# FFN weights split by ScalarE and GpSimd and turned by DMA during the attention; shared groups one unit per slot in steps 16 to 18

## The chip, the cores and the metric

The kernel runs on one core of one Trainium2 chip. The metric is the device time in microseconds of one execution. The core has TensorE (PE: matrix products, and transposes as products with an identity), VectorE (DVE), ScalarE (ACT), GpSimd (POOL) and SyncE (SP, which in this kernel issues nearly all DMAs). Each engine runs its own program in order. They wait for each other on semaphores alone, and every wait, buffer and address is written out by hand.

## The reference

64 sequences of 64 tokens of width 128 (4096 tokens), each with a context of 128 rows. All in float32:

```python
x = x + xattn(layernorm(x), ctx)      # 16 heads of 8, then Wo, layer norm with gamma and beta
x = x + attn(layernorm(x))            # one causal head of 128, then Wo
x2n = layernorm(x)
gates, idx = top_k(x2n @ gate_w.T, 2); gates = softmax(gates)       # 8 experts
shared   = silu(x2n @ shared_w1.T) @ shared_w2.T                    # hidden width 512
selected = sum over the two experts e of a token:
           gate * (silu(x2n @ experts_w1[e].T) @ experts_w2[e].T)   # hidden width 512
x = x + shared + selected
```

The 18 weight matrices of the last part (8 experts and the shared one, two each) have 128x512 elements. The products of the FFN need them with the other dimension on the partitions than they have in memory, so each must be transposed ("turned"), and each is kept as two float16 tiles, a high part W_hi and a rest W_lo, scaled by 256. A product of the FFN is three float16 products: W_hi by x_hi, W_hi by x_lo, W_lo by x_hi.

## The kernel before, in words

The tokens stand in 32 tiles of 128, two tiles to a **half** (four sequences), so there are 16 halves. **Step** h of the attention works on half h: `most_steps` calls `step` for h from -3 to 17, and step 18 is called by itself. A step has eight **slots** (`UNITS`), two heads in each: TensorE makes the scores twice (once for the row maximum, DVE's `m_bf` L902, and once transposed for the exponential), ScalarE makes the exponential `p` (L680) and its float16 part `p_hi` (L685), and the rest `p_lo` (L356) is made by POOL in slots 1, 4 and 6 (`ON_POOL`) and by DVE in the others. POOL takes up its part at the start of the slot after. Around this, the slots do smaller work for other halves, each piece at a fixed slot in the table `MISC`: the transposes and projections of halves h+1 and h+2, output and layer norm of half h-1 (`yn`, `x1n`, `x1T`), and the second attention of half h-2 (`qk`, `s`, `pT`, `z`). The layer norms' roots run on POOL (`root`, L524 and L526) and the normalised rows are made by DVE (L805). In steps 16, 17 and 18 there are no scores any more, and only this smaller work is left, a chain in which each engine hands on to the next. Its last result is `x2n` of half 15, which step 18 makes: a high and a low part, turned by two DMA transposes into `x2T`.

SP's queue, for half h (`turn`): x rows two halves ahead, the context one ahead, then `q_parts` to DRAM (L390), the two halves of `k_parts` to DRAM (L393), and 16 pairs of small loads that bring them back stacked by head (`Qs` L408, `Ks` L409); between these, `x2_rows` turns `x2n` of an older half (L424).

Routing is done in four parts of the tokens, after steps 11, 15 and 17 and, for the last four tiles (part `LAST`), after step 18: TensorE makes the logits (L1203) and counts ranks, DVE works out for each token the two rows `row_no` of a list in DRAM, and POOL sends the tokens' rows there, 64 indirect DMAs in all (L537), 56 of them in the slots of steps 11 to 18 (table `SENT`), eight at the end. SP writes padding rows behind each expert's list (L470), from places that DVE has worked out (`pad0`), and then fetches blocks of 256 rows, transposing them into `xT` (L481).

The FFN runs in **units** of 128 of the 512 hidden columns: "up" is 3 products of 512 columns on TensorE (L1311), silu (L742) and `h_hi` (L745) on ScalarE, `h_lo` (L991) on DVE, and "down" is 12 products of 128 columns on TensorE (L1324). A unit's up stands three units (`AHEAD`) before its down in TensorE's order. The shared expert has 8 groups of 512 tokens with 4 units each (32 units); the routed part has 40 blocks of 256 rows with 2 units each (each unit then takes 256 of the hidden columns). POOL scatters a block's result to DRAM (L617, the 80 indirect DMAs), and it is read back (`yt`) and added at the end.

The 18 weights are loaded by SP, turned by TensorE in steps 16 and 17, four products each (L1235), into four PSUM banks; ScalarE writes W_hi from there (L658) and DVE W_lo (L812). `weights_at` says which matrices belong to a slot: one a slot at first, then two. Then come the first two shared groups (8 units), step 18, the routing of the last part, 16 more shared units, the 80 routed units, and the last 8 shared units.

## Time and profile before

| | |
|---|---|
| median of 3 runs | 634.56 us (634.42 to 635.3) |
| the profiled execution | 632.83 us |
| its span (first to last instruction) | 631.1 us |
| busy: TensorE, VectorE, ScalarE, GpSimd | 481.8, 469.4, 399.6, 336.7 us |
| mean granted clock of TensorE | 0.917 of full speed |

The 1.7 us between the profiled execution and its span lie before the first and behind the last instruction. No engine is busy for the whole span: the busy shares are means over stages that have different limits, so the kernel must be read stage by stage. The attention steps 0 to 15 take from about 40 to 389 us, steps 16 to 18 with the routing behind them from there to about 456, and the routed part from about 480 to the end.

### The profile page before, as it was taken

The page shows a single profiled execution, that of the slowest core. Times are in us where ns is not written, and L with a number is a line of the kernel's source. Part 1 is how long each engine was busy: PE and PEld are TensorE (multiplying, and loading weights), DVE is VectorE, ACT ScalarE, POOL GpSimd, SP SyncE. Part 2 cuts the span into 40 slices and gives each one's busy share as a digit, 9 for nine tenths or more (in the row PEclk, how much of TensorE's full clock was granted, in tenths as well). Part 3 has the DMA queues.
Part 4 walks back from the last instruction along what each step waited for, and adds up shares of the span by engine and source line. Part 5 has one row for each costly group of instructions (what it writes and reads, how often), then busy time and mean ns, then how long its engine had stood idle before and what let it go on. Part 6 is the DMA issues. An engine that isn't in the chain of part 4 may idle for free.

```text
span 631.1 us, 18436 instructions
## 1 busy us (share of the span) xinstructions
PE 481.8 (76%) x5770; PEld 396.6 (63%) x5770; DVE 469.4 (74%) x1417; ACT 399.6 (63%) x767; POOL 336.7 (53%) x486
## 2 busy tenths in 40 slices
PE   4488888778877887858877776558579999999960
PEld 1277677666666666646665665455358888888840
DVE  4258999998899999977877878575566666666644
ACT  2257777766777677644666653346669888888840
POOL 2213554355346444525777775755041888878842
PEclk9998999998999999976889986777879999999985
DMA  3453433444354455322543500344132453534349
GB/s 100 109 126 80 115 103 98 96 99 109 96 100 97 98 103 102 95 72 60 109 101 94 130 31 22 116 132 122 27 103 48 93 95 82 96 72 91 45 128 273
DMA packets 166703, 61.09 MB, mean 97 GB/s; under 512 B 116547, under 2 KB 163415, under 8 KB 166628
## 3 DMA queue, kind: packets, MB, share of 16 engines
q1 hardware_dynamic: 161968, 51.65, 36.1%
q0 software_dynamic: 4640, 8.48, 4.9%
q8 instruction: 42, 0.69, 0.5%
q14 instruction: 33, 0.27, 0.2%
q10 hardware_dynamic: 20, 0.01, 0.0%
HBM read 28.40 MB, written 23.28 MB: 82 GB/s over the span
## 4 chain that ended last, share of the span: by engine, by line
PE 31%; DVE 23%; issue 19%; POOL 13%; SPq 4%; ACT 4%; DMA 3%; DVEq 1%; POOLq 0%; ACTq 0%
PE bank L1311 8%; PE bank L1324 7%; DVE p_lo L356 3%; POOL listed L537 3%; DVE O_tok L887 3%; DVE m_bf L902 2%; POOL results L617 2%; POOL rstd L526 2%; PE bank L1160 2%; DVE st L794 2%; POOL p_lo L356 2%; PE bank L1151 2%; PE bank L1288 1%; SPq L408 1%; PE bank L1269 1%
## 5 line engine op out<-in xcount | busy, mean ns | idle before, releaser
L680 ACT ACTIVATE p<-bank 128x512 f32<-128x512 f32 x128 | 76.2, 595 | 60.8 <-PE bank L1255 26.2
L991 DVE TENSOR_TENSOR h_lo<-h,h_hi 128x512 f16<-128x512 f32 x112 | 77.3, 692 | 42.7 <-ACT h_hi L745 41.7
L902 DVE TENSOR_REDUCE m_bf<-bank 128x4 bf16<-128x512 f32 x128 | 86.9, 679 | 22.4 <-PE bank L1269 21.3
L1324 PE MATMUL bank<-W_hi,h_hi 128*128 (+1 forms) x448 | 83.1, 222 | 13.7 <-DVE h_lo L991 13.7
L617 POOL DMA_INDIRECT results<-y_sb,row_info x80 | 79.3, 991 | 19.4 <-issue 17.6
L356 POOL TENSOR_TENSOR p_lo<-p,p_hi 128x512 f16<-128x512 f32 x48 | 56.7, 1181 | 56.2 <-ACT p_hi L685 55.9
L537 POOL DMA_INDIRECT listed<-rows_of,row_no x64 | 63.9, 998 | 38.9 <-DVE row_no L875 23.5
L685 ACT ACTIVATE p_hi<-p 128x512 f16<-128x512 f32 x128 | 80.6, 630 | 5.5
L1324 PE MATMUL bank<-W_lo,h_hi 128*128 (+1 forms) x448 | 82.7, 222 | 0.0
L1324 PE MATMUL bank<-W_hi,h_lo 128*128 (+1 forms) x448 | 82.7, 222 | 0.0
L742 ACT ACTIVATE h<-bank 128x512 f32<-128x512 f32 x112 | 66.7, 596 | 23.7 <-PE bank L1311 18.9
L524 POOL TENSOR_TENSOR vpe<-mv,eps 128x2 f32<-128x2 f32 x64 | 15.1, 236 | 112.3 <-DVE mv L798 112.1
L745 ACT ACTIVATE h_hi<-h 128x512 f16<-128x512 f32 x112 | 70.5, 630 | 3.5
L1288 PE MATMUL bank<-V_hi,p_hi 128*128 128x17 f16 x512 | 51.1, 174 | 19.2 <-POOL p_lo L356 12.5
L1311 PE MATMUL bank<-xT,W_hi 128*128 128x256 f16 x320 | 57.1, 274 | 3.8 <-ACT h L742 1.9
L1288 PEld LDWEIGHTS bank<-V_hi,p_hi 128*128 128x128 f16 x512 | 42.9, 98 | 26.4 <-POOL p_lo L356 15.5
L356 DVE TENSOR_TENSOR p_lo<-p,p_hi 128x512 f16<-128x512 f32 x80 | 57.6, 720 | 0.7 <-ACT p_hi L685 0.7
L1324 PEld LDWEIGHTS bank<-W_hi,h_hi 128*128 128x128 f16 x448 | 44.4, 99 | 20.1 <-issue 15.3
L1269 PE MATMUL bank<-Ks,Qs 128*128 128x128 f16 x512 | 52.8, 230 | 4.3 <-DMA Ks<-k_rows 4.3
L1250 PEld LDWEIGHTS bank<-neg_ident,m_bf 128*128 128x128 bf16 x512 | 42.4, 104 | 18.6 <-issue 5.2
L1250 PE MATMUL bank<-neg_ident,m_bf 128*128 128x128 bf16 x512 | 53.3, 231 | 0.6 <-DVE m_bf L902 0.6
L1255 PE MATMUL bank<-Qs,Ks 128*128 128x256 f16 x256 | 52.6, 290 | 0.0
(198 smaller groups left out, 1367.0 us busy)
## 6 DMA issues: line engine op xcount, KB each, us to landing
k_rows<-k_parts SPq DMA_DIRECT2D x32, 256.0 KB, 2.7
Ks<-k_rows SPq DMA_DIRECT2D x128, 64.0 KB
ctx_in<-in_ctx SPq DMA_DIRECT2D x16, 256.0 KB, 3.2
Qs<-q_rows SPq DMA_DIRECT2D x128, 32.0 KB
w_in<-in_L_ffn_experts_w SPq DMA_DIRECT2D x16, 256.0 KB, 4.3
yt<-results SPq DMA_DIRECT2D x16, 256.0 KB, 5.2
x_all<-in_x SPq DMA_DIRECT2D x16, 128.0 KB, 2.7
q_rows<-q_parts SPq DMA_DIRECT2D x16, 128.0 KB, 2.0
```

Of the source, the lines that this page charges most:

```text
L356: eng.tensor_tensor(p_lo[:, s % 4, :], p32[:, s % 2, :], p_hi[:, s % 4, :], ALU.subtract).then_inc(low_of(h, s)[0], 1)
L537: pool.indirect_dma_start(out=listed[:, :], out_offset=bass.IndirectOffsetOnAxis(ap=row_no[:, n, t:t + 1], axis=0), in_=rows_of[:, t, n, : ...
L617: pool.indirect_dma_start(out=results[:, :], out_offset=bass.IndirectOffsetOnAxis(ap=row_info[b][:, t, 0:1].bitcast(U32), axis=0), in_=y_s ...
L680: act.activation(p32[:, s % 2, :], T_ps[s % 2][:, :], ACT.Exp, scale=XSCALE).then_inc(exp_done, 1)
L685: act.activation(p_hi[:, s % 4, :], p32[:, s % 2, :], ACT.Copy).then_inc(p_hi_done, 1)
L745: act.activation(h_hi[k % RING][:, :], h32[k % RING][:, :], ACT.Copy).then_inc(hhi_done, 1)
L902: dve.tensor_reduce(m_bf[:, slot, :], M_ps[s % 2][:, :].rearrange("p (n k) -> p n k", k=SK), AX.X, ALU.max).then_inc(max_done, 1)
L991: dve.tensor_tensor(h_lo[k % RING][:, :], h32[k % RING][:, :], h_hi[k % RING][:, :], ALU.subtract).then_inc(hlo_done, 1)
L1250: pe.matmul(T_ps[s % 2][:, n * P:n * P + P], m_bf[:, r * UNITS + s, n:n + 1].broadcast_to([P, P]), neg_ident[:, :], start=(n == 0), stop=F ...
L1288: last = pe.matmul(PV_ps[p][:, hd * VW:hd * VW + VW], pp[:, sv % 4, w0:w0 + P], vv[rv][:, p, hd, :], start=(m == 0), stop=(m == 2))
L1311: last = pe.matmul(U_ps[k % RING][:, c * width:c * width + width], ww[:, w(c)], xx[part], start=(m == 0), stop=(m == 2))
L1324: last = pe.matmul(y[:, t * D:t * D + D], hh[k % RING][:, cols], ww[:, w(c)], start=(first and c == 0 and t == 0 and m == 0), stop=(end an ...
```

## The change

- **Loading and turning.** TensorE's transposes, their PSUM banks and the two evacuations are gone. From step -1 on, each step takes one matrix: SP loads it (`load_weight`, into one of two `w_in` buffers), ScalarE scales it in place at the end of slot 1 (`weights_scaled`) and makes the float16 part at the end of slot 6 (`weights_hi`), POOL makes the rest at slot 7, behind its `p_lo` of slot 6 and ahead of `xb`, and two steps later SP turns both by two DMA transposes of 128x512 float16 (`turn_weight`), between the context load and the writes of q and k. The 18 steps are -1 to 16. The shared expert's two matrices are first (`W_ORDER`).
- **Shared units.** From slot 3 of step 16 on, each slot ends with one shared unit on TensorE, ScalarE and DVE: units 0 to 4 in step 16, 5 to 12 in step 17, 13 to 20 in step 18 (`shared_at`, `FILL_FROM`, `FILLED` = 21). Units 21 to 31 follow; the logits of the last part stand behind unit 23, the ranks behind 25, DVE's stages of routing behind 23, 24, 25 and 26 (`ROUTE_AT`). All 32 come ahead of the routed blocks, and none is left behind them.
- **SP's tables.** Padding waits for `pad0` alone, which DVE now makes first, and SP loads eight registers with one instruction (`rows_at`) instead of one before each DMA.
- **End.** After the last block DVE goes straight to the sums of the read-back results.

```diff
-WEIGHTS_FROM = HALVES * 8 + 2
+WEIGHTS_AT = 1
+FILL_FROM = HALVES * UNITS + 3
+FILLED = (HALVES + 3) * UNITS - FILL_FROM
+ROUTE_AT = (23, 24, 25, 26)
+W_ORDER = (2 * E, 2 * E + 1) + tuple(range(2 * E))
...
-        w_in = sb("w_in", [P, 4, CH, P])
+        w_in = sb("w_in", [P, 2, CH, P])
+        w_split = sb("w_split", [P, 2, 2, HID], F16)
...
+        def weight_step(h):
+
+            return not isinstance(h, int) or 0 <= h + WEIGHTS_AT < 2 * NE
+
+        def weight_ring(h, r):
+
+            return (1 - r, 8 * h + (8 * r + 16), 16 * h + 16 * r)
+
+        def shared_at(h, s):
+
+            n = h * UNITS + s - FILL_FROM if isinstance(h, int) else -1
+            return range(n, n + 1) if n >= 0 else range(0)
...
+            def load_weight(k):
+                e, second = weight_of(k)
+                w = ((ew1, ew2)[second][e] if e < E else (sw1, sw2)[second])
+                need(sp, wt_lo, k - 1)
+                sp.dma_start(w_in[:, k % 2, :, :],
+                             w.rearrange("d (c h) -> d c h", h=P) if second else w.rearrange("(c p) d -> p c d", p=P)
+                             ).then_inc(w_loaded[k % 2], 16)
+
+            def turn_weight(k):
+
+                e, second = weight_of(k)
+                sp.wait_ge(wt_lo, k + 1)
+                for part, dst in enumerate(((W2_hi, W2_lo) if second else (W1_hi, W1_lo))):
+                    sp.dma_start_transpose(dst[:, e * HID:e * HID + HID].rearrange("p (c n) -> p c n", c=CH),
+                                           w_split[:, k % 2, part, :]).then_inc(turned[k % 2], 16)
...
+                if h >= 2:
+                    turn_weight(h - 2)
+                load_weight(h)
...
+                    if s == 7 and weight_step(h):
+                        q = weight_ring(h, r)[0]
+                        pool.wait_ge(wt_hi, h + (WEIGHTS_AT + 1))
+                        pool.tensor_tensor(w_split[:, q, 1, :], w_in[:, q, :, :].rearrange("p c d -> p (c d)"),
+                                           w_split[:, q, 0, :], ALU.subtract).then_inc(wt_lo, 1)
...
+            def weights_scaled(h, r):
+
+                q, loads, turns = weight_ring(h, r)
+                act.wait_ge(w_loaded[q], loads)
+                act.activation(w_in[:, q, :, :], w_in[:, q, :, :], ACT.Copy, scale=WSCALE).then_inc(wt_scaled, 1)
+
+            def weights_hi(h, r):
+
+                q, loads, turns = weight_ring(h, r)
+                act.wait_ge(wt_scaled, h + (WEIGHTS_AT + 1))
+                need(act, turned[q], turns)
+                act.activation(w_split[:, q, 0, :], w_in[:, q, :, :].rearrange("p c d -> p (c d)"),
+                               ACT.Copy).then_inc(wt_hi, 1)
...
-                    for n in weights_at(h, s):
-                        weights_hi(n)
+                    if s == 1 and weight_step(h):
+                        weights_scaled(h, r)
+                    if s == 6 and weight_step(h):
+                        weights_hi(h, r)
+                    for n in shared_at(h, s):
+                        unit(n, n)
...
+            def rows_at(table_, last):
+
+                return nc.values_load_multi_w_load_instructions(table_, engines=[mybir.EngineType.SP], min_val=0, max_val=last)[1]
...
-            sp.wait_ge(tables_ready, 3)
-            for e in range(E):
-                first = sp.value_load(pad0[0:1, e:e + 1], min_val=0, max_val=E * REGION - BR)
+            sp.wait_ge(tables_ready, 1)
+            for first in rows_at(pad0[0:1, 0:E], E * REGION - BR):
...
+                firsts = rows_at(row0[0:1, i * LB:i * LB + LB], E * REGION)
+                for b, first in enumerate(firsts):
...
+            for n in range(FILLED, ROUTE_AT[3] + 1):
+                shared_unit(n)
+                for stage in {ROUTE_AT[0]: (0,), ROUTE_AT[1]: (1,), ROUTE_AT[2]: (2, 3), ROUTE_AT[3]: (5,)}.get(n, ()):
+                    route(LAST, stage)
...
+            block_out(BLOCKS // LB - 1, LB - 1)
+            for g in range(FG):
+                routed_in(g)
...
-            def weights(n):
-
-                pe.wait_ge(w_loaded[n % 4], 16 * (n // 4 + 1))
-                need(pe, wt_lo, n - 3)
-                if n < 4:
-                    pe.wait_ge(max_done, UNITS * HALVES)
-                    pe.wait_ge(norm_done, PAIRS * HALVES)
-                for c in range(CH):
-                    last = pe.transpose(W_ps[n % 4][:, c * P:c * P + P], w_in[:, n % 4, c, :], ident[:, :])
-                last.then_inc(wt_pe, 1)
...
+                if n == 0:
+                    pe.wait_ge(exp_done, UNITS * HALVES)
+                    pe.wait_ge(max_done, UNITS * HALVES)
+                    pe.wait_ge(norm_done, PAIRS * HALVES)
+                    for r in range(2):
+                        pe.wait_ge(turned[r], 32)
+                    for ahead in range(AHEAD):
+                        shared_up(ahead)
...
-            pe.wait_ge(exp_done, UNITS * HALVES)
-            pe.wait_ge(wt_lo, 2 * NE)
-            for n in range(AHEAD):
-                shared_up(n)
-            shared_before(0, EARLY * CH)
             step(HALVES + 2, 0)
-
-            pe.wait_ge(x2T_in, 32 * HALVES)
-            for name in ("x1T", "z"):
-                pe.wait_ge(ev[name], HALVES)
-            logits(LAST)
-            ranks(LAST)
-            shared_before(EARLY * CH, N0)
+            for n in range(FILLED, N0):
+                shared_unit(n)
+                if n == ROUTE_AT[0]:
+                    pe.wait_ge(x2T_in, 32 * HALVES)
+                    for name in ("x1T", "z"):
+                        pe.wait_ge(ev[name], HALVES)
+                    logits(LAST)
+                if n == ROUTE_AT[2]:
+                    ranks(LAST)
```

The two loops `for n in shared_at(h, s)` stand at the same place, the end of a slot, in the programs of TensorE, ScalarE and DVE; on TensorE and DVE they call `shared_unit`.

How the order moves, at three places. **POOL, from slot 7 of step 15 to the root of the output norm in step 16**, before. `xb` is half 15's residual with a bias, the L537 rows are sends, `yg` and `x_1` belong to half 15:

```order
L356 TENSOR_TENSOR p_lo<-p,p_hi 128x512 [waits v_done,p_hi_done]
L574 TENSOR_TENSOR xb<-x_all,bcast 128x256 [waits x1_done,x_in]
L537 DMA listed<-rows_of,row_no 35072x130 [waits placed,rows_copied]
L537 DMA listed<-rows_of,row_no 35072x130
L524 TENSOR_TENSOR vpe<-mv,eps 128x2 [waits normed_x2,stat_x2]
L526 TENSOR_TENSOR rstd<-vpe,minus_half 128x2 [waits vpe_x2]
L537 DMA listed<-rows_of,row_no 35072x130 x6
L524 TENSOR_TENSOR vpe<-mv,eps 128x2 [waits normed_y,stat_y]
L526 TENSOR_TENSOR rstd<-vpe,minus_half 128x2 [waits vpe_y]
```

The same place after (L555 are the sends):

```order
L360 TENSOR_TENSOR p_lo<-p,p_hi 128x512 [waits v_done,p_hi_done]
L574 TENSOR_TENSOR w_split<-w_in,w_split 128x512 [waits wt_hi]
L597 TENSOR_TENSOR xb<-x_all,bcast 128x256 [waits x1_done,x_in]
L555 DMA listed<-rows_of,row_no 35072x130 [waits placed,rows_copied]
L555 DMA listed<-rows_of,row_no 35072x130
L542 TENSOR_TENSOR vpe<-mv,eps 128x2 [waits normed_x2,stat_x2]
L544 TENSOR_TENSOR rstd<-vpe,minus_half 128x2 [waits vpe_x2]
L555 DMA listed<-rows_of,row_no 35072x130 x6
L542 TENSOR_TENSOR vpe<-mv,eps 128x2 [waits normed_y,stat_y]
L544 TENSOR_TENSOR rstd<-vpe,minus_half 128x2 [waits vpe_y]
L580 TENSOR_TENSOR yg<-yn,bcast 128x256 [waits normed_y]
L586 TENSOR_TENSOR x_1<-yg,xb 128x256 [waits ev_z,normed_x1,xb_done,yg_done]
```

The subtraction of one weight now stands between `p_lo` and `xb`, ahead of all the sends; it waits for ScalarE (`wt_hi`). In steps 0 to 14 it stands at the same place, between `p_lo` and `xb`.

**ScalarE, second half of step 17**, before. `V`, `P`, `rows_of` and `P2T` are pieces of the second attention and the norm, `second_exp` belongs to the gates:

```order
L668 ACTIVATE V<-bank 128x256 [waits mm_v2,mm_z]
L658 ACTIVATE W_hi<-bank 128x512 [waits wt_pe]
L664 ACTIVATE second_exp<-gates 128x4 [waits gate_step]
L658 ACTIVATE W_hi<-bank 128x512 [waits wt_pe]
L712 ACTIVATE P,rs<-sm,nbias 128x128 [waits mm_pT,nbias_done]
L712 ACTIVATE P,rs<-sm,nbias 128x128
L717 ACTIVATE rows_of<-x2n 128x2x128 [waits normed_x2]
L658 ACTIVATE W_hi<-bank 128x512 [waits wt_pe]
L668 ACTIVATE P2T<-bank 128x256 [waits mm_pT,mm_z]
L658 ACTIVATE W_hi<-bank 128x512 [waits wt_pe] x8
```

and after:

```order
L699 ACTIVATE V<-bank 128x256 [waits mm_v2,mm_z]
L777 ACTIVATE h_2<-bank 128x512 [waits hlo_done,u_done]
L780 ACTIVATE h_hi<-h_2 128x512 [waits d_done,silu_done]
L695 ACT_TABLE_LOAD
L695 ACTIVATE second_exp<-gates 128x4 [waits gate_step]
L777 ACT_TABLE_LOAD [waits hlo_done]
L777 ACTIVATE h_3<-bank 128x512 [waits u_done]
L780 ACTIVATE h_hi<-h_3 128x512 [waits d_done,silu_done]
L743 ACT_TABLE_LOAD [waits mm_pT]
L743 ACTIVATE P,rs<-sm,nbias 128x128 [waits nbias_done]
L743 ACTIVATE P,rs<-sm,nbias 128x128
L748 ACTIVATE rows_of<-x2n 128x2x128 [waits normed_x2]
```

Between two of these pieces there is now a silu and a cast to float16, where before there was one evacuation of a weight. Silu and the exponential want different tables, so there is a table load at each change of function: seven from step 16 on by this listing, three before.

**SP, behind the last `x2_rows`**, before:

```order
L465 DMA listed<-padding 128x2x130 [waits consts_pool]
L469 TENSOR_LOAD pad [waits tables_ready]
L469 ISA x2
L470 ISA
L470 DMA listed<-padding 128x2x130
L469 TENSOR_LOAD pad
L469 ISA x2
L470 ISA
L470 DMA listed<-padding 128x2x130
```

and after:

```order
L485 DMA listed<-padding 128x2x130 [waits consts_pool]
L482 TENSOR_LOAD pad [waits tables_ready]
L482 ISA x16
L489 ISA
L489 DMA listed<-padding 128x2x130
L489 ISA
L489 DMA listed<-padding 128x2x130
```

One load fills the registers for all eight padding writes, and the wait ahead of it is met by the first table. The fetches (L501) are loaded the same way, eight at a time.

## Rows read from the trace of the kernel before

**Rows 1.** Busy time by stage; columns as in the header, clock and DMA share last.

```profile
core 0: us, PE busy (x) PEld busy (x) DVE busy (x) ACT busy (x) POOL busy (x), PEclk, DMA share, GB/s
200.00:300.00 100.00, 76.93 (x1000) 64.11 (x999) 88.04 (x325) 62.95 (x135) 45.03 (x65) 0.91 0.43 89
...
400.00:420.00 20.00, 12.58 (x72) 11.23 (x72) 12.46 (x55) 9.04 (x24) 15.86 (x21) 0.66 0.54 152
420.00:440.00 20.00, 13.02 (x71) 8.34 (x72) 12.12 (x41) 10.96 (x21) 8.48 (x11) 0.74 0.41 122
...
520.00:560.00 40.00, 38.70 (x491) 34.02 (x492) 26.56 (x55) 33.24 (x55) 32.96 (x40) 1.00 0.45 90
```

**Rows 2.** Timeline of DVE in step 8; start, us, engine, line, [idle before <- releaser].

```profile
216.55 1.85 DVE L805 TENSOR_SCALAR x1n<-x,mv,rstd 128x128 f32<-128x128 f32 x2
...
219.44 0.58 DVE L805 TENSOR_SCALAR xn<-x_all,mv,rstd 128x128 f32 x2
```

**Rows 3.** Timeline of POOL in the same stretch.

```profile
217.18 1.15 POOL L356 TENSOR_TENSOR p_lo<-p,p_hi 128x512 f16<-128x512 f32 x1
218.28 0.72 POOL L574 TENSOR_TENSOR xb<-x_all,bcast 128x256 f32<-128x256 f32 x1
220.80 0.19 POOL L524 TENSOR_TENSOR vpe<-mv,eps 128x2 f32<-128x2 f32 x1 [1.80 <-DVE mv L798]
```

**Rows 4.** Timeline of the start: POOL and PE.

```profile
22.84 0.19 POOL L602 CAST fills<-fills_i 1x16 f32<-1x16 int32 x1
31.31 1.03 PE L1269 MATMUL bank<-Ks,Qs 128*128 128x128 f16 x8 [4.31 <-DMA Ks<-k_rows]
```

**Rows 5.** SP: its waits (total, times, longest), then its timeline in step 8.

```profile
SPq L393 <- DVE k_parts L943: 72.0, 15, 6.8
SPq L390 <- DVE q_parts L929: 26.8, 13, 5.8
...
214.34 2.52 SPq L424 DMA_TRANSPOSE x2T<-rows_of  x2
```

**Rows 6.** Timeline of steps 16 to 18: POOL, PE and DVE.

```profile
404.70 0.72 POOL L526 TENSOR_TENSOR rstd<-vpe,minus_half 128x2 f32<-128x2 f32 x1
411.16 0.66 PE L1175 MATMUL bank<-ident,x1n 128*128 128x128 f32 x2 [6.02 <-DVE x1n L805]
425.95 1.23 PE L1196 MATMUL bank<-V,P2T 128*128 128x128 f32 x4 [1.63 <-DVE row_at L863]
446.32 0.60 DVE L805 TENSOR_SCALAR x2n<-x_all,mv,rstd 128x128 f32<-128x128 f32 x2
451.51 0.19 PE L1203 MATMUL bank<-gate_hi,x2T 128*128 128x8 f16 x1 [2.63 <-DMA x2T<-rows_of]
```

**Rows 7.** Timeline of ACT and DVE: one unit of the early groups, and the table loads behind them.

```profile
441.00 0.58 ACT L742 ACTIVATE h<-bank 128x512 f32<-128x512 f32 x1
442.27 0.69 DVE L991 TENSOR_TENSOR h_lo<-h,h_hi 128x512 f16<-128x512 f32 x1 [0.46 <-ACT h_hi L745]
453.09 1.28 ACT L742 ACT_TABLE_LOAD   x1
454.39 0.60 ACT L742 ACTIVATE h<-bank 128x512 f32<-128x512 f32 x1
```

**Rows 8.** POOL, SP and PE from the last rank to the first routed unit.

```profile
457.17 0.96 POOL L537 DMA_INDIRECT listed<-rows_of,row_no  x1 [16.52 <-DVE row_no L875]
466.24 0.96 POOL L537 DMA_INDIRECT listed<-rows_of,row_no  x1 [0.30 <-issue]
462.10 9.15 SPq L470 DMA_DIRECT2D listed<-padding  x8
473.83 1.25 SPq L481 DMA_TRANSPOSE xT<-listed  x1
479.67 0.38 PE L1311 MATMUL bank<-xT,W_hi 128*128 128x256 f16 x2
```

**Rows 9.** The chain that ended last: the landing of an indirect write.

```profile
604.60 2.10 DMA results<-y_sb,row_info
```

More of the change, by code:

```diff
@@ L751, in _ @@
             most_steps(act, step, setup)
-            for n in range(EARLY * CH):
+            step(HALVES + 2, 0)
+            for n in range(FILLED, N0):
                 unit(n, n)
-            step(HALVES + 2, 0)
-            second_weight(LAST)
-            for n in range(EARLY * CH, N0):
-                unit(n, n)
+                if n == ROUTE_AT[2]:
+                    second_weight(LAST)
             routed(0, False)
@@ L762, in _ @@
             routed(BLOCKS // LB - 1, True)
-            for n in range(N1, NU):
-                unit(n, n)
         @block.vector
@@ L983, in step @@
                         route(beside(h), s)
[L984 to L985 removed]
+                    for n in shared_at(h, s):
+                        shared_unit(n)
             def unit(n, k):
```

146 lines of the change are left out of this document (50 added, 96 removed).

## The prediction

> **What bounds the kernel now.** I read the windows by stage first, since the mean shares of the page mix stages. Up to step 15 DVE is the fullest engine (88 of 100 us, PE 77, POOL 45); in steps 16 to 18 nobody is full (PE 13 of 20, DVE 12, ACT 9 to 11) and the granted clock is 0.66 to 0.74; in the routed part PE is full (38.7 of 40) at clock 1.00 [rows 1]. So the attention goes by DVE, the middle by a chain of handoffs, the end by PE.
>
> Then the timelines. The middle has these milestones: root of half 15's output norm at 404.70, `x1T` of half 15 at 411.16, `z` of half 15 at 425.95, `x2n` at 446.32, last logits at 451.51 [rows 6], first send of the last part at 457.17, last send at 466.24, first fetch at 473.83, first routed unit on PE at 479.67 [rows 8]. `x2n` waits for nothing: it stands in DVE's order behind eight early units (one starts silu at 441.00 and ends `h_lo` at 442.96 [rows 7]). Its statistics were ready about 12 us earlier, 8.5 us behind `z`, by my reading of the order. From 479.67 to the end of the span (631.1) are 151.4 us. Those are 80 routed units at PE's pace, then 8 shared units beside the read-back, which waits for the last scatter to land [rows 9]; the read-back, not those units, ends the kernel.
>
> **The change, part by part.** The sum is made on the span, 631.1; the profiled execution was 632.83 (1.7 more) and the median of the runs is 634.56 (1.7 more again).
>
> *Start.* POOL's first subtraction stands ahead of its setup, which ends at 22.84 + 0.19 now, and waits for a matrix that step -1 scales and casts at about 28. Some 3.5 us of setup then come behind it: POOL is done at about 32.9 instead of 23.0. PE's setup starts behind the product at 31.31 that waited 4.31 for a DMA [rows 4], so of the 10 us only **+0.8** is left. Bounds 0 and 3.5.
>
> *Attention, POOL and DVE.* The subtraction has the form of `p_lo`: 1.15 us. In step 8 it takes 218.3 to 219.45, and moves `xb` from 218.28 to 219.45. The following wait, 1.80 before 220.80, covers it on POOL [rows 3]. But DVE's `x1n` pair took 1.85 beside POOL's `x1b` and `p_lo`, and the same form (`xn`) 0.58 with POOL idle: 1.27 lost to POOL's presence [rows 2]. After the change `xb` lies on `xn`. I take 0.25 a step (a fifth of that 1.27, since DVE loses only where both want the same thing at the same moment) for the 11 steps 0 to 10: **+2.7**. Bounds: 0, and 1.15 a step over 18 steps, 20.7. The Trainium skill ("GPSIMD Engine Reference", Key points) says that GpSimd shares its SBUF interfaces with VectorE and contends with it when VectorE runs in a two-port mode or has two SBUF inputs. By that rule many neighbours of the subtraction would stall and not `xn` alone; the 1.85 against 0.58 agrees with a stall. It is the third case below.
>
> *Attention, ACT.* Two evacuation-like operations of 0.6 a step. ACT is under two thirds busy and its waits hide them: 0.
>
> *Attention, SP.* Two transposes (1.26 each, as 2.52 for two), one load (about 0.5): 3 us a step. SP waits in total 26.8 for `q_parts` and 72.0 for `k_parts` [rows 5], together 6.6 in each of 15 steps. The new work stands right ahead of these waits: 0. If a transpose of 128x512 took more than about 3.7 us, `q_rows` would be late, then the stack, then the scores. The nearest row has 128x128 blocks too, so I take 1.26, and keep the double (2.5) as upper end, still hidden.
>
> *Step 16.* POOL is paced by sends up to the root at 404.70. One subtraction (step 15's) stands ahead of them: +1.15. PE's `x1T` at 411.16, slot 7, then stands behind shared unit 3, whose silu, cast, rest and down are 2.6 in a row (1.96 from 441.00 to 442.96 [rows 7] and 0.67 of down), of which some 1.9 is left: together **+3.0**. Call its new time X = 414.2.
>
> *Step 17 to the last rank.* In each slot the order is now: piece on PE, its evacuation on ACT or DVE, silu, cast, rest, down, and only then the next piece. That is 2.6 for the unit and about 0.7 for the piece: 3.3. From `x1T` to `z` there are six slots (7, 0 to 4): 19.8. ACT also changes its table four more times in all; the row has 1.28 for a load and the next activation 1.30 behind its start [rows 7]: 5.1. So `z` at X + 24.9; before it was 14.8 behind `x1T`. The statistics follow at X + 28.5, `x2n` one slot on, X + 31.7. Its turn and the units up to 23, 11 units at about 1.15 each, the pace of ACT's two operations: logits at X + 44.5, against 451.51 - 411.16 = 40.35 before. Then 8.0 instead of 4.9 to the last `row_no`, as units 24 to 26 stand between the stages: X + 52.5, against 456.4 - 411.16 = 45.2: **+7.3**. Gone against before are the 28 transposes of weights in this stretch and the eight units ahead of `x2n`; come are 13 units in the slots.
>
> The Trainium skill ("ScalarE: Activation LUTs", What ACT_TABLE_LOAD costs) gives a table switch about 1.28 us and 1.38 for a drain, 2.66 together. The row has the next activation 1.30 behind the load's start, so the trace doesn't show the drain there. By the page, an estimate, four switches would be 10.6 instead of 5.1: 5.4 more than my sum.
>
> *Fetching.* Before, last rank (456.4) to first fetch (473.83) took 17.45, since padding (462.10 + 9.15) ended behind the sends. Padding now waits for an early table and one load, and is over before the sends are. Left is: 0.7 to the first send, 10.1 for eight (457.17 to 467.20), 2.1 for the landing of the last ([rows 9] has 2.10 for the same kind), 0.7 to load registers: 13.6, **-3.85**. Bounds -5 and 0 (if landing takes as long as the padding did).
>
> *First routed unit.* From 473.83 to 479.67 are 5.84, of which the fetch's own landing is 2.6 (busy DMAs till about 476.4); the rest was PE still at its shared units. In the changed kernel PE is through with them, and waits: **-3.2**. It then starts after some 9 us of idleness; the granted clock in idle stretches is 0.66 to 0.74 [rows 1], so the first blocks run slower: **+1.3** (0 to 3).
>
> *End.* Without the last eight units the read-back still decides: **-0.5**.
>
> **Sum:** 0.8 + 2.7 + 3.0 + 7.3 - 3.85 - 3.2 + 1.3 - 0.5 = +7.6. Span 638.7, profiled execution 640.4, median 642.2. As low clocks in the longer chain are priced at nothing, I say 642.5.
>
> **The rivals.**
> 1. *The forecast*: slots in series. 636 to 649. Chance 0.45.
> 2. *The other side, faster*: the units hide in the waits of steps 16 and 17. PE, ACT and DVE are each only half busy there [rows 1], and a unit could lie beside the piece rather than behind it. For this: a unit's up is issued three units early. Against: down waits for its own `h_lo`, and the next piece stands behind it. Price: if a slot takes 2.4 instead of 3.3 and the table loads fall into waits, six slots give -5.4, loads -5.1, the two slots to `x2n` and the logits -3: the last rank at X + 39 instead of X + 52.5, so -13.5 on my sum: 628.6. It decides from about 2.7 a slot downward. 622 to 633. Chance 0.27.
> 3. *DVE loses to POOL's subtraction every time*: up to 1.15 by 18 steps, or at the least 0.6 each. For it: 1.85 against 0.58 [rows 2]. Against: it is one pair. 11 to 21 more less the 2.7: 650 to 656. In steps 11 to 15 POOL's own sends pace it too, 5 by 1.15 = 5.8 at most. Chance 0.18.
> 4. *SP late*: transposes slower than 3.7, delaying `q_rows` each step. At 1 us a step, +16: about 658. Chance 0.05.
> 5. *Nothing*: gain and loss cancel, 633.3 to 635.8. Chance 0.05.
>
> **How the numbers follow.** Predicted 642.5. The range 629 to 653 leaves out about half of case 2 (0.1), the upper half of case 3 and case 4: 2 in 10. The likeliest case's own range is 636 to 649. About 0.2% (1.3 us) is what a measurement of this kernel can tell from no change. Faster: case 2, 0.27. Same: case 5 and a little of the edges, 0.06. Slower: the rest, 0.67.
>
> **What the changed profile would show.** Right: 11 steady steps longer by 0.1 to 0.5 each, with `xn` longer; `x1T` of half 15 near 417; `z` near 442; from `x1T` to `z` PE waits mostly for DVE's `h_lo`; last rank near 470; first fetch 13 to 14 behind it; PE idle for 8 us or more ahead of the first routed unit; 150 to 152 us from that unit to the end. Wrong: pieces and units side by side, `z` less than 18 behind `x1T` (case 2); DVE's small operations at 1.8 in most steps (case 3); PE waiting for `Ks` or `Qs` in each step (case 4). A surprise would be a span from first routed unit to the end that differs by more than 2 us, since I take the routed part as unchanged.

## The result and the profile after

The changed kernel takes 655.75 us (median of 4 runs, 653.53 to 655.9) against 634.49 for the kernel before on the same chip. The ratio is 1.0341, 95% interval 1.0308 to 1.0375: slower by 21 us. The profiled execution took 655.9, its span is 653.7, 22.6 more than the span before. The forecast was 642.5 with 629 to 653: the sign was right, the size was not.

The page of the changed kernel begins, and its windows by stage are (columns as in [rows 1]):

```profile
span 653.7 us, 18292 instructions
...
PE 480.0 (73%) x5667; PEld 391.4 (60%) x5698; DVE 467.7 (72%) x1399; ACT 410.8 (63%) x789; POOL 359.6 (55%) x504
```

```profile
245.88:266.84 20.96, 16.77 (x228) 13.99 (x228) 19.99 (x63) 16.00 (x34) 11.30 (x17) 1.00 0.61 123
...
420.00:440.00 20.00, 13.94 (x96) 8.76 (x95) 8.88 (x39) 9.94 (x16) 9.67 (x11) 0.67 0.15 38
440.00:460.00 20.00, 15.43 (x132) 11.08 (x131) 11.58 (x37) 14.85 (x29) 6.97 (x8) 0.73 0.11 31
...
480.00:500.00 20.00, 4.12 (x28) 3.06 (x29) 6.08 (x15) 1.77 (x3) 7.33 (x7) 0.53 0.55 89
520.00:560.00 40.00, 38.65 (x496) 33.94 (x494) 26.90 (x56) 33.44 (x55) 33.44 (x42) 1.00 0.46 86
```

PE's busy time hardly moved (481.8 to 480.0). The turning of the 18 weights on PE (72 products) is gone, and yet steps 16 and 17 are as empty as before: from 420 to 440 DVE has less work than in [rows 1] (8.88 against 12.12) and PE hardly more (13.94 against 13.02). Between 480 and 500 PE is busy for 4 of 20 us at clock 0.53, a hole that the kernel before had no room for. A granted clock of 0.50 is the lower of TensorE's two levels (1.2 GHz) and 1.00 the upper (2.4 GHz); a value between them is the mean of a stretch. The routed part is as it was.

The milestones, as timeline rows of the changed kernel:

```profile
422.47 0.39 PE L1192 MATMUL bank<-ident,x1n 128*128 128x128 f32 x2
450.77 1.17 PE L1213 MATMUL bank<-V,P2T 128*128 128x128 f32 x4
456.93 0.60 DVE L837 TENSOR_SCALAR x2n<-x_all,mv,rstd 128x128 f32<-128x128 f32 x2
471.31 0.17 PE L1220 MATMUL bank<-gate_hi,x2T 128*128 128x8 f16 x1
478.49 0.17 DVE L900 CAST row_no<-row_f 128x4 uint32<-128x4 f32 x1
...
488.37 0.96 POOL L555 DMA_INDIRECT listed<-rows_of,row_no  x1 [0.30 <-issue]
...
481.95 4.90 SPq L489 DMA_DIRECT2D listed<-padding  x8
496.45 1.25 SPq L501 DMA_TRANSPOSE xT<-listed  x1
...
499.88 0.61 PE L1317 MATMUL bank<-xT,W_hi 128*128 128x256 f16 x2 [12.67 <-DMA row_info<-listed]
```

Set against [rows 6, 8] this gives the bill. The last rank before was at 456.74, the start of the second of the two casts. The prediction took 456.4, which is the end of the first (456.22 + 0.17): that moves 0.3 between two of its terms and changes no sum.

| stretch | before | after | difference | forecast |
|---|---|---|---|---|
| start, to the first exponential of step 0 | 39.5 | 40.3 | +0.8 | +0.8 |
| steps 0 to 14 | 328.3 | 334.3 | +5.9 | +2.7 (called attention) |
| step 15 and 16, to `x1T` of half 15 | 43.3 | 47.9 | +4.6 | +3.0 |
| `x1T` to last rank | 45.6 | 56.0 | +10.4 | +7.3 |
| last rank to first fetch | 17.1 | 18.0 | +0.9 | -3.85 |
| first fetch to first routed unit | 5.8 | 3.4 | -2.4 | -3.2 |
| first routed unit to the end | 151.4 | 153.8 | +2.4 | +0.8 |

### The profile page after: what moved, and what is told of

Read it like the earlier page. It is cut to its first block, busy times and chain, and to the rows that moved or that the text cites. A ratio compares the mean times of both kernels' runs of the same rounds, so it can differ in the third digit from the quotient of the medians.

```text
span 653.7 us, 18292 instructions
## 1 busy us (share of the span) xinstructions
PE 480.0 (73%) x5667; PEld 391.4 (60%) x5698; DVE 467.7 (72%) x1399; ACT 410.8 (63%) x789; POOL 359.6 (55%) x504
## 4 chain that ended last, share of the span: by engine, by line
PE 40%; DVE 22%; issue 15%; POOL 10%; ACT 7%; DMA 2%; SPq 1%; DVEq 1%; POOLq 0%; ACTq 0%
PE bank L1317 11%; PE bank L1330 11%; POOL listed L555 4%; DVE p_lo L360 3%; DVE O_tok L912 3%; PE bank L1177 2%; POOL rstd L544 2%; PE bank L1168 2%; DVE m_bf L927 2%; PE bank L1294 2%; DVE st L826 2%; PE bank L1256 2%; PE bank L1261 2%; PE bank L1174 2%; DVE x1n L837 1%
## 5 line engine op out<-in xcount | busy, mean ns | idle before, releaser
L711 ACT ACTIVATE p<-bank 128x512 f32<-128x512 f32 x128 | 75.9, 593 | 50.4 <-POOL p_lo L360 24.1
L1330 PE MATMUL bank<-W_hi,h_hi 128*128 (+1 forms) x448 | 86.4, 227 | 18.6 <-DVE h_lo L1016 18.6
L555 POOL DMA_INDIRECT listed<-rows_of,row_no x64 | 66.4, 1037 | 51.1 <-DVE row_no L900 35.9
L1330 PE MATMUL bank<-W_lo,h_hi 128*128 (+1 forms) x448 | 86.0, 227 | 0.0
L1330 PE MATMUL bank<-W_hi,h_lo 128*128 (+1 forms) x448 | 86.0, 227 | 0.0
L1330 PEld LDWEIGHTS bank<-W_hi,h_hi 128*128 128x128 f16 x448 | 45.6, 102 | 30.4 <-issue 15.6
L360 DVE TENSOR_TENSOR p_lo<-p,p_hi 128x512 f16<-128x512 f32 x80 | 60.7, 758 | 0.7 <-ACT p_hi L716 0.7
```

The lines of the kernel that those rows point to most:

```text
L360: eng.tensor_tensor(p_lo[:, s % 4, :], p32[:, s % 2, :], p_hi[:, s % 4, :], ALU.subtract).then_inc(low_of(h, s)[0], 1)
L555: pool.indirect_dma_start(out=listed[:, :], out_offset=bass.IndirectOffsetOnAxis(ap=row_no[:, n, t:t + 1], axis=0), in_=rows_of[:, t, n, : ...
L711: act.activation(p32[:, s % 2, :], T_ps[s % 2][:, :], ACT.Exp, scale=XSCALE).then_inc(exp_done, 1)
L1330: last = pe.matmul(y[:, t * D:t * D + D], hh[k % RING][:, cols], ww[:, w(c)], start=(first and c == 0 and t == 0 and m == 0), stop=(end an ...
```

## The experiments

The times below are medians, each with its ratio to runs of the kernel before on the same chip. Those runs had medians of 634.5 to 635.0.

### e2_one_by_one: registers loaded one by one

```diff
-            for first in rows_at(pad0[0:1, 0:E], E * REGION - BR):
+            for e in range(E):
+                first = sp.value_load(pad0[0:1, e:e + 1], min_val=0, max_val=E * REGION - BR)
...
-                firsts = rows_at(row0[0:1, i * LB:i * LB + LB], E * REGION)
-                for b, first in enumerate(firsts):
+                for b in range(LB):
...
+                    first = sp.value_load(row0[0:1, one(i * LB + b)], min_val=0, max_val=E * REGION)
```

> The changed kernel, but SyncE loads one register ahead of each padding write and each fetch, as the kernel before did; padding still starts at the first table. Theory (the first fetch pays for loading eight registers at once, and eight padding writes in 4.9 us fill the DMA engines under the last sends): the first fetch comes about 3 us earlier behind the last send, 652 to 653 us. Rival (the sends' own landing takes the 7 us whatever SyncE does): no change, 655.5. Second rival: the loads return inside the routed loop and delay fetches there, over 656.

648.86 us, ratio 1.0228 (1.0172 to 1.0285), 3 below the 652 to 653 that was expected. From the last rank (477.25) to the first fetch are 13.58 us instead of 17.96, 4.4 less. SP's wait for the sends, in the changed kernel and in this one:

```profile
SPq L493 <- DMA listed<-rows_of,row_no: 6.8, 1, 6.8
```

```profile
SPq L494 <- DMA listed<-rows_of,row_no: 2.7, 1, 2.7
```

and this kernel's last send, its padding, and its first fetch:

```profile
487.14 0.96 POOL L556 DMA_INDIRECT listed<-rows_of,row_no  x1 [0.30 <-issue]
...
479.92 7.45 SPq L490 DMA_DIRECT2D listed<-padding  x7
490.83 1.25 SPq L502 DMA_TRANSPOSE xT<-listed  x1
```

The two causes can be read apart. In the changed kernel the padding is issued up to 486.85 and SP then waits 6.8, to 493.65. The last send was issued by 489.33, so it took 4.3 to land. The fetch at 496.45 comes 2.8 later, which is the load of eight registers. Here the padding ends at 487.37, the wait at 490.07, 2.0 behind the send's issue (488.10), and the fetch follows 0.76 later. So 2.3 us went to a send that landed late under eight padding writes issued in 4.9 us, and 2.0 to the bulk load ahead of the first fetch. The DMAs were loaded accordingly, here the changed kernel and then this one (the DMA share is the last number but one):

```profile
484.00:490.00 6.00, 3.21 (x22) 2.12 (x19) 2.25 (x4) 1.23 (x2) 4.21 (x4) 0.50 1.19 156
...
480.00:488.00 8.00, 4.00 (x27) 2.92 (x27) 4.91 (x12) 1.23 (x2) 6.27 (x6) 0.51 0.55 157
```

The median padding write took 5.4 us from issue to landing in the changed kernel and 3.1 in this one, while all DMAs together moved as much (156 and 157 GB/s). The spans differ by 6.7. The rest of that is 1.3 up to `x1T`, which no edit of this kernel reaches, and 1.1 behind the first routed unit.

### b1_early_pad: the kernel before, padding at the first table

```diff
-            sp.wait_ge(tables_ready, 3)
+            sp.wait_ge(tables_ready, 1)
             for e in range(E):
...
             sp.wait_ge(padded, 16 * (E + 1))
+            sp.wait_ge(tables_ready, 3)
```

> The kernel before, and only the padding starts at the first table (still one register per DMA). Theory (TensorE is at its 16 shared units until 479.4, so an earlier fetch only waits): first fetch 3 to 3.5 us earlier behind the last rank, first routed unit unmoved, 634 us. Rival (the fetch sets the routed start): 631.

634.23 us, ratio 0.9982 (0.9953 to 1.0011). From rank to fetch are 13.85 us instead of 17.1, and the first routed unit comes 9.58 behind the fetch instead of 5.84: 23.4 and 22.9 from the rank. An early fetch is worth nothing as long as PE has 16 units to do.

### e1_lo_slot3 and e5_lo_behind_x2n: GpSimd's subtraction moved

```diff
-                    if s == 7 and weight_step(h):      # GpSimd
+                    if s == 3 and weight_step(h):
+                        if not isinstance(h, int) or 3 <= h < HALVES + 3:   # e5 alone
+                            pool.wait_ge(normed["x2"], h * 2 + (-4))
...
-                    if s == 6 and weight_step(h):      # ScalarE, weights_hi
+                    if s == 2 and weight_step(h):
```

> The changed kernel, but ScalarE makes the float16 part of the weight at the end of slot 2 and GpSimd subtracts at slot 3, where it stood idle for about 5 us, and no longer between p_lo and xb. Theory (the subtraction pushes xb onto VectorE's xn, which takes 1.01 instead of 0.58): xn back at 0.59, each attention step shorter by 0.4, over 16 steps 6 to 7 us: about 649 us instead of 655.75. Rival (ScalarE's two pieces or the extra DMAs lengthen the step): xn may fall, the step doesn't, 655 to 656.

> As e1_lo_slot3 (float16 part at slot 2, subtraction at slot 3), but GpSimd waits for VectorE's x2n first, so that the subtraction lies beside q_parts, m_bf and p_lo and beside no TENSOR_SCALAR. Theory (only VectorE's TENSOR_SCALAR normalisations from SBUF are held by a 512-wide GpSimd operation; e1 moved the hold from xn, 1.01 to 0.59, to x2n, 0.59 to 1.5): both at 0.59, steps 0 to 10 back to 20.9 us, total 655.75 less 5 to 6: about 650. Rival (ScalarE's cast in slot 2 is what made e1 slow): steps stay at 22 to 24, 660 or more.

e1 took 662.2 us, ratio 1.0434 (1.0377 to 1.0491), 6 slower than the changed kernel: the total was missed on the wrong side. The rows say where the hold went. First the changed kernel in step 8 (DVE, then POOL), the answer to [rows 2, 3]:

```profile
221.22 1.86 DVE L837 TENSOR_SCALAR x1n<-x,mv,rstd 128x128 f32<-128x128 f32 x2
...
224.12 1.01 DVE L837 TENSOR_SCALAR xn<-x_all,mv,rstd 128x128 f32 x2
...
221.85 1.15 POOL L360 TENSOR_TENSOR p_lo<-p,p_hi 128x512 f16<-128x512 f32 x1
222.96 1.15 POOL L574 TENSOR_TENSOR w_split<-w_in,w_split 128x512 f16<-128x512 f32 x1
224.07 0.72 POOL L597 TENSOR_TENSOR xb<-x_all,bcast 128x256 f32<-128x256 f32 x1
```

then e1 (DVE, POOL):

```profile
215.37 1.51 DVE L837 TENSOR_SCALAR x2n<-x_all,mv,rstd 128x128 f32 x2
...
229.34 0.59 DVE L837 TENSOR_SCALAR xn<-x_all,mv,rstd 128x128 f32 x2
...
215.65 1.15 POOL L574 TENSOR_TENSOR w_split<-w_in,w_split 128x512 f16<-128x512 f32 x1 [1.74 <-ACT w_split L688]
```

`xn` is back at 0.59, and `x2n`, 0.59 in the changed kernel, takes 1.51, because the subtraction now lies on it. `x2n` stands ahead of `q_parts`, on which PE waits. That accounts for 0.9 us a step: the step from 207.90, at a granted clock of 1.00, took 21.95, where the same step took 21.02 before. The steps from 135.99 to 207.90 took 23.8 to 24.1 at a clock of 0.86, where before they took 21.2 to 22.0 at 0.96 to 1.00. This is the larger part of e1's loss, and why the clock fell there is not shown. e5 lets the subtraction wait until `x2n` is over:

```profile
229.72 0.59 DVE L839 TENSOR_SCALAR x2n<-x_all,mv,rstd 128x128 f32 x2
...
221.87 0.59 DVE L839 TENSOR_SCALAR xn<-x_all,mv,rstd 128x128 f32 x2
...
230.39 1.16 POOL L576 TENSOR_TENSOR w_split<-w_in,w_split 128x512 f16<-128x512 f32 x1 [2.13 <-DVE x2n L839]
```

Both are at 0.59, and e5 took 646.94 us, ratio 1.0186 (1.0138 to 1.0235), 3 below the 650 that was expected, with ScalarE's cast still in slot 2. So the hold is between GpSimd's wide operation and what VectorE does at that moment, and nothing else of the move. While it lay beside e5's subtraction, `q_parts` took 0.48, as it did without it (0.47). The `p_lo` that VectorE makes, with two inputs from SBUF, was held: the one at 231.22, which meets the end of the subtraction (231.55), took 0.88 instead of 0.68, and the step was no longer for it.

The rows also show how long a hold is. The first `xn` of the changed kernel's pair ran from 224.12 to 224.88, 0.09 behind the end of `xb` (224.79), and the second took its usual 0.34. e1's `x2n` ended at 216.88, 0.08 behind the subtraction (216.80), and `x1n` before at 218.40, 0.07 behind `p_lo` (218.33). In these places the held operation ends when GpSimd's does, so the loss is what is left of GpSimd's operation, and not a share of it. From [rows 2, 3], with `xb` moved to 219.45 and `xn` at 219.44, this gives about 0.5 a step. Of steps in which the granted clock was 1.00 the one from 240.79 took 20.53 before, the one from 245.88 took 20.96 in the changed kernel, and the one from 243.22 took 20.51 in e5: 0.43 a step, which is what `xn` lost (1.01 less 0.58). Steps 4 and 9, at 1.00 in all three kernels, show the same: 20.98, 21.43 and 21.00, and 20.84, 21.26 and 20.84. The 8.8 us between the changed kernel and e5 are more than this explains. Its span is 8.2 shorter: 2.7 by the start of step 15, 0.4 more by `x1T`, 2.4 from there to the rank, 1.2 to the fetch, 1.5 at the end. Only the first two lie where the subtraction was. The 2.4 and the 1.5 go with a higher granted clock: from `x1T` to `z` it was 0.87 in e5 and 0.64 in the changed kernel, from `z` to the rank 1.00 and 0.94, and from the first routed unit to the first scatter 0.86 and 0.75. Why the clock differed, and the 1.2, is not tracked down.

### e3_units_after: weights in the attention, units out of the slots

```diff
-FILL_FROM = HALVES * UNITS + 3
-ROUTE_AT = (23, 24, 25, 26)
+FILL_AT = {HALVES + 1: (0, 0, 0, 0, 0, 0, 0, 8)}     # units at the end of each slot
+ROUTE_AT = (7, 7, 7, 7)                              # logits and ranks right behind step 18
```

> The weights alone: they are split and turned during the attention as in the changed kernel, but shared units 0 to 7 run behind step 17, then step 18, logits and ranks of the last part, then units 8 to 31. Theory (the units in the slots make each slot a series of handoffs): from x1T of half 15 to its z 14 us or less instead of 28.3, x2n held back by the eight units as before, last rank 40 to 44 behind x1T instead of 56; but 24 units (some 31 us) now stand ahead of the first routed one where 21 us are wanted, so 10 us are given back: 643 to 648 us. Rival (clock and turned weights, not the slots, are what costs): last rank still over 50 behind x1T, 655 or more.

640.36 us, ratio 1.0112 (1.0075 to 1.015). `z` is 11.9 behind `x1T` (28.3 in the changed kernel, 14.8 before), the last rank 35.3 (56.0, 45.6), and the first routed unit comes 33.8 behind the rank, since 24 units stand between. The total was 3 below the range given. The mechanism is as expected: against before, with 8 units ahead of the rank in both, the weights part shortens the way to it by 10.3. One unit a slot, and the 27 units that stand ahead of the last rank in the changed kernel, lengthen it by 20.7.

### e4_route_early: four units less in step 18, logits earlier

```diff
+FILL_AT = {HALVES: (0, 0, 0, 1, 1, 1, 1, 1), HALVES + 1: (1, 1, 1, 1, 1, 1, 1, 1),
+           HALVES + 2: (1, 1, 1, 1, 0, 0, 0, 0)}
-ROUTE_AT = (23, 24, 25, 26)
+ROUTE_AT = (16, 17, 18, 19)
```

> The changed kernel, but slots 4 to 7 of step 18 take no unit (17 done by its end instead of 21), and logits, stages and ranks of the last part stand behind units 16, 17, 18 and 19 instead of 23 to 26. Theory (x2T of the last half is there at 461 and its logits stand behind units until 471): logits 8 to 9 us earlier, last rank too, the units left over fill part of PE's idle 12.7 us ahead of the first routed unit: 646 to 648 us. Rival (the routed part starts when its lists are full and something else than the ranks sets that): 654 to 656.

644.04 us, ratio 1.012 (1.0054 to 1.0186). The logits stand at 462.20 instead of 471.31, and wait 0.39 for `x2T`. The last rank is at 469.25 instead of 478.49, the first routed unit at 489.86. It took 2 us less than expected. In the changed kernel `x2T` was ready, and its logits stood 9 us behind units that PE had idle time for later.

### g1_grouped and g2_two_slots_free: what a unit in a slot costs

```diff
+FILL_AT = {HALVES: (0, 0, 0, 0, 0, 0, 5, 0), HALVES + 1: (0, 0, 0, 6, 0, 0, 0, 2), HALVES + 2: (1,) * 8}   # g1
...
+FILL_AT = {HALVES: (0, 0, 0, 1, 1, 1, 1, 1), HALVES + 1: (1, 1, 0, 0, 1, 1, 1, 1), HALVES + 2: (1,) * 8}   # g2
```

> The changed kernel with the same 21 units by the end of step 18, but grouped: 5 in slot 6 of step 16, where TensorE waits 6 us for x1n, 6 in slot 3 and 2 in slot 7 of step 17, then one a slot in step 18 as before. One table switch pair less. Theory (one unit a slot is a handoff in series, about 2.7 us each; grouped units run at ScalarE's pace, about 1.2 each): z of half 15 about 20 to 22 us behind its x1T instead of 28.3, last rank 47 to 50 behind instead of 56: 647 to 650 us. Rival (it is the units' work itself, or the low clock, however they are placed): z still 27 or more, 655.

> The changed kernel, but slots 2 and 3 of step 17, where ScalarE makes exponentials between two silus, take no unit (19 done by the end of step 18; the ranks stay behind unit 25). Two units and one pair of table loads less between x1T and z. Theory (each unit in a slot costs its handoffs, about 2.7, and each table load its 1.28): z 20 to 22 behind x1T instead of 28.3, two units given back later at 1.3 each, 649 to 652 us. Rival (the loads hide, a unit costs 1.2): z 25 to 26, 655.

g1: 651.24 us, ratio 1.0237 (1.0208 to 1.0265). g2: 649.73 us, ratio 1.0227 (1.018 to 1.0274). `x1T` and `z` in g1, then in g2:

```profile
429.68 0.39 PE L1197 MATMUL bank<-ident,x1n 128*128 128x128 f32 x2
450.18 0.68 PE L1218 MATMUL bank<-V,P2T 128*128 128x128 f32 x4 [0.58 <-DVE row_at L891]
```

```profile
418.82 0.39 PE L1197 MATMUL bank<-ident,x1n 128*128 128x128 f32 x2
440.54 1.16 PE L1218 MATMUL bank<-V,P2T 128*128 128x128 f32 x4
```

g1 ended just above the 647 to 650 that was expected, g2 within its range. With two units and two table loads less, g2 has `z` 6.6 earlier (21.7 instead of 28.3). With the load at 1.28 a unit in a slot costs (6.6 - 2.56) / 2 = 2.0. From no unit (11.9 in e3) to six units and four loads (28.3) are 16.4, so (16.4 - 5.1) / 6 = 1.9 a unit. Both differences agree. g1 has six units in one slot and one pair of loads, and `z` at 20.5. That is 8.6 more than e3: 2.6 for the loads and 1.0 for each unit, near the 1.15 from one silu of a group to the next (442.14 and 443.29 before). These prices are good to some tenths only, since the granted clock in this stretch was 0.50 in e3, 0.64 in the changed kernel, 0.77 in g2 and 0.83 in g1.

But g1's `x1T` came 7.2 us later than in the changed kernel. Its five units were meant to hide in a wait of PE, and didn't:

```profile
PE bank L1335 <- DVE h_lo L1019: 6.2, 1, 6.2
```

The wait was that of DVE too. Its order has `x1n` (418.73) ahead of the units' `h_lo` (420.12), so PE's first down waited for the same root of the layer norm as `x1T` would have, and then four more downs stood ahead of `x1T`.

### f1_weights_only, f2_weights_clear, h1_mid_group, h2_three_last: the part that is worth having

f1 is the kernel before with the weights part of the change, without the shared units in slots, without bulk loads, padding as in b1. f2 adds e5's placement. h1 adds:

```diff
             step(HALVES + 2, 0)
+            shared_before(EARLY * CH, (EARLY + MID) * CH)    # MID = 1; so on PE and DVE, and ACT
...
-            shared_before(EARLY * CH, N0)
+            shared_before((EARLY + MID) * CH, N0)
```

h2 has `EARLY = 1` and `BEFORE = 5` as well (4 units behind step 17, 4 before the logits, 12 behind the ranks, 12 at the end), with the PSUM bank of a routed block shifted by one.

> The kernel before with only the weights part of the change (split during the attention, turned by DMA) and its own order of the FFN: units 0 to 7 behind step 17, 16 behind the ranks, 8 at the very end; padding starts at the first table, one register per DMA. Theory (the slots and the bulk loads are what costs; the weights part costs 5 to 6 us in the attention and gives back 10 in the middle, as in e3_units_after): last rank about 35 behind x1T, first fetch 13.6 behind it but PE busy with 16 units until 21, so 5.5 plus 10 less: 629 to 632 us. Rival (turned weights cost in the middle too): 635 to 640.

> f1_weights_only with the subtraction placed as in e5_lo_behind_x2n. Theory: 5 us less than f1, 624 to 627. Rival (the cast in slot 2 costs): more than f1.

> f2_weights_clear with units 8 to 11 between x2n and the last logits, where TensorE waits 5.2 us for the turned x2T, and 12 units behind the ranks instead of 16. Theory (16 units behind the ranks are 6 us more than the fetch needs): first routed unit 18 to 19 behind the last rank instead of 23.5; the table load of second_exp shows, 1.3: 625 to 627 us. Rival (the four units delay the logits by as much as they save): 629.

> h1_mid_group with one group less behind step 17 (units 0 to 3), the four units of the group moved to the end, so that 12 instead of 8 run behind the routed blocks, beside the read-back. Theory (x2n is held only by the units ahead of it, and the end by the read-back): x2n 4.6 us earlier, the end unmoved: 621 to 623 us. Rival (four more units at the end show there, 5 us): 626 to 628.

| kernel | us | ratio to before (interval) | rank behind `x1T` | first fetch behind rank | first routed unit behind fetch |
|---|---|---|---|---|---|
| f1_weights_only | 630.94 | 0.9955 (0.9927 to 0.9983) | 35.4 | 13.65 | 9.66 |
| f2_weights_clear | 629.44 | 0.9877 (0.9816 to 0.9938) | 35.2 | 13.77 | 9.72 |
| h1_mid_group | 626.14 | 0.9873 (0.9816 to 0.9931) | 36.2 | 13.46 | 4.47 |
| h2_three_last | 620.52 | 0.9780 (0.9730 to 0.9830) | 32.4 | 13.91 | 3.66 |

The rows of f1 that carry the argument:

```profile
418.89 0.66 PE L1193 MATMUL bank<-ident,x1n 128*128 128x128 f32 x2 [8.72 <-DVE x1n L832]
430.82 1.19 PE L1214 MATMUL bank<-V,P2T 128*128 128x128 f32 x4 [0.58 <-issue]
...
454.27 0.17 DVE L895 CAST row_no<-row_f 128x4 uint32<-128x4 f32 x1
...
467.92 1.25 SPq L493 DMA_TRANSPOSE xT<-listed  x1
...
477.58 0.38 PE L1316 MATMUL bank<-xT,W_hi 128*128 128x256 f16 x2
```

f1 alone is a little faster than before, by 0.2 to 0.7%, though its attention is 5.2 us longer, and its total lies in the expected 629 to 632. f2, at 629.44, missed the expected 624 to 627. By the medians it gained 1.5 against f1 instead of 5; by the two ratios 0.8%, which is 5, but their intervals meet (0.9927 and 0.9938). So the size of this gain is open. Of its steps 3 to 10 those at clock 1.00 took 20.5 to 21.0, as before, but two had clock 0.87 and 0.88 and took 22.7, so the gain from placement isn't seen whole. h1 came within its range, and h2 ended 0.5 below its own: first routed unit at 463.54, 16 us earlier than before, and 153.3 from there to the end.

## Why the prediction was right or wrong

The forecast range ended at 653, and the median was 655.75. The one term whose path was wrong, and which turned a gain into a loss, is the fetching: with it as forecast, 4.8 us less, the time would have been 651.0. The other terms missed by 10 us together, all of them in size.

**Right.** Slower, by units in series in the slots. From `x1T` to `z` PE waits 9.8 us for `h_lo`, in six waits, as the prediction said it would. The start was forecast to the tenth, and by its own path: POOL's setup ends at 32.79, forecast 32.9. The subtraction took 1.15 and pushed `xb` onto `xn`, as the step on POOL and DVE said. Scaling and casting on ScalarE cost nothing in the steps at full clock: e5 has both in its 20.51 us, against 20.53 before. SP's transposes took 1.22 and 1.26 in most steps, as forecast, and stayed hidden: SP still waits 49.7 us for `k_parts` in the changed kernel and 4.2 for `q_parts` (72.0 and 26.8 in [rows 5]), 45 less, the 3 us a step of the forecast. The table loads were priced rightly at what the row has. In the changed kernel:

```profile
434.92 1.28 ACT L695 ACT_TABLE_LOAD   x1
436.22 0.20 ACT L695 ACTIVATE second_exp<-gates 128x4 f32<-128x4 f32 x1
436.44 1.28 ACT L777 ACT_TABLE_LOAD   x1
```

The activation is 1.30 behind the load's start, and the next load starts 0.02 behind the activation's end (436.42). The Trainium skill ("ScalarE: Activation LUTs", What ACT_TABLE_LOAD costs) adds 1.38 of drain to a switch; these rows have no room for it.

**Wrong: fetching, -3.85 forecast, +0.9 measured (4.8 of the 15 us missed).** The term took 2.1 for the last send's landing, from a scatter at the end of the kernel where nothing else was on the queues, and 0.7 for the load of registers, from loads of one. In the changed kernel they are 4.3 and 2.8. Both come from parts of the change that the term itself listed, and the result lies outside the term's own bounds of -5 and 0. e2 takes out the bulk load and the burst and has 13.58, where the forecast had said 13.6. That "padding is over before the sends are" was right; that it leaves their landing alone was the failed step.

**Wrong in size: the attention, +2.7 forecast, +5.9 measured.** The mechanism was right, its price was 0.43 a step and not 0.25, since `xn` is held until `xb` ends. Nine pairs of `xn` in a row, of steps 2 to 10, took 1.01 or 1.02 instead of 0.59. That is 4.7 over the 11 steps 0 to 10, and 4.8 was measured there, but in part by luck: step 3 ran at a granted clock of 0.92 (22.05 us) against 1.00 (20.53) before and step 7 at 0.96 against 1.00 (22.30 and 21.19), and steps 0 and 6 were 0.58 and 0.45 shorter. The other 1.2 lies in steps 11 to 14, for which the term had nothing.

**Wrong in size: `x1T` to the last rank, +7.3 forecast, +10.4 measured.** The sum had the unit at 2.6 in series and the piece at 0.7. Measured are 1.9 for the unit and 2.0 for the pieces (11.9 over six slots). The errors cancel in part: `z` was forecast at 24.9 and came at 28.3. Behind it `x2n` took 6.2 (6.8 forecast), the logits 14.4 more (12.8) and the rank 7.2 more (8.0). The table loads at 1.28 each were right. The low clock, "priced at nothing" by the prediction, has a share: with the same units in the slots `z` came 28.2 to 28.3 behind `x1T` at a granted clock of 0.64 (the changed kernel, e2 and e4), 27.6 at 0.69 (e1) and 26.7 at 0.87 (e5). In e1 and e5 the last subtraction had moved too, so the share isn't measured by itself. The prediction's "28 transposes" in this stretch are 52 products, of 13 weights; its sum doesn't use them.

**Wrong in size: step 16, +3.0 forecast, +4.6 measured.** e3, with the subtraction and without units, has 1.7 of it (`x1T` 45.0 behind the start of step 15, before 43.3), so the units took 2.9, where 1.9 was said.

**Right in kind: the first routed unit, -3.2 forecast, -2.4 measured.** PE was through with its units and waited, but the fetch took 3.4 to serve it and not 2.6.

**The end: +0.8 forecast, +2.4 measured.** The prediction itself called more than 2 us here a surprise. All of it lies before the first block's result is scattered. That scatter is issued 8.34 behind the first routed unit before and 10.93 in the changed kernel; from it to the end are 143.1 and 142.9. PE has no wait in either stretch:

```profile
479.67:488.01 8.34, 8.34 (x115) 7.90 (x113) 5.58 (x10) 7.72 (x14) 0.67 (x2) 1.00 0.28 50
499.88:510.81 10.93, 10.93 (x112) 9.84 (x113) 4.69 (x8) 6.96 (x12) 0.67 (x2) 0.75 0.42 73
```

By PE's order it is the same work (some products are missing from each trace), at a granted clock of 0.75 instead of 1.00. So the term for the clock behind an idle PE was 2.6 and not 1.3 (within its 0 to 3), and dropping the last eight units gave 0.2 and not 0.5. The seven kernels whose PE had run out of units and waited for the first fetch (the changed one, e1, e2, e4, e5, g1, g2) have their first scatter at 9.7 to 10.9; those whose PE came straight from shared units, well behind the fetch (before, b1, e3, f1, f2), at 8.3, all five. h2 needs 9.7 at a clock of 1.00: it starts so close behind the fetch that PE waits 1.2 for the second block's rows.

**The rivals.** Case 2 (units hide beside the pieces) has fallen: `z` is 28.3 behind `x1T`. Case 3 (the hold every time, 11 to 21 us) has the right kind of cause, but a hold of 0.43. Its time, 650 to 656, contains the result by luck, for another reason. Case 4 has fallen (PE waits for `Ks` once, 4.5 us, as it did before with 4.3), and so has case 5.

**Still open.** Why some attention steps are granted a lower clock, and whether splitting weights there makes it more frequent: before, three of steps 1 to 10 were below 1.00, in the changed kernel six, in e5 two. Runs of one kernel spread by 8 us and more (f2: 623.43 to 631.29; the kernel before in one series: 630.14 to 638.86), so the intervals of f2 and h1 overlap, and between those two only the rows of the milestones show the gain.

## What to carry to other kernels

Work moved into an engine's idle time is hidden only if no other engine in its chain stands at the same wait. Where steps are handed over in series, each added unit costs its own full handoff (1.9 us here, against 1.0 in a group), so put units where one engine alone waits for a DMA, in a group, and ask what stands behind them. When a change has several parts, split it by its terms: here the turning of the weights shortened the middle by 10 us, and the filling of the slots, with the late ranks, lengthened it by 21. The turning alone (f1) is worth 3 to 4 us, since it made the attention 5 longer and PE had 16 units to do ahead of the routed part in any case. And ask of a faster transfer what it now collides with: padding issued in one burst held up the sends that the fetch was waiting for.

## What the runs showed of the hardware that was not expected

- VectorE's `TENSOR_SCALAR` from SBUF (128x128, two of them, 0.59 us) took 1.01, 1.51 and 1.86 us beside 512- and 256-wide GpSimd operations, and the hold followed the GpSimd operation wherever that was moved. The held operation ended 0.07 to 0.09 behind GpSimd's. `q_parts`, which reads PSUM and SBUF, took 0.47 or 0.48 in all 16 steps of e5, beside the subtraction as well; the one exception is in e1 (1.56 at 316.78, directly behind a held `x2n`), and it isn't explained. The Trainium skill ("GPSIMD Engine Reference", Key points) names VectorE's two-port mode and two SBUF inputs as the cases. The trace agrees that VectorE is held, and that `p_lo` on VectorE, with two SBUF inputs, is held too (0.88 instead of 0.68); which operations run in a two-port mode is not shown by any run here.
- Loading eight registers of SyncE at once delayed the first use by 2.8 us, against 0.76 for one.
- The landing of an indirect write, from the end of its issue to the end of SP's wait, took 2.0 us behind padding writes issued one by one (DMA share 0.55), and 4.3 with eight of 130 KB each issued in 4.9 us (1.19).
- The routed part's first stretch, the same 112 to 115 products with PE never waiting, took 8.34 us at a granted clock of 1.00, 9.68 at 0.86 (e5) and 10.93 at 0.75.
